# Another order and split of the first blocks, and a later start of GpSimd's gathers, in a kernel of two LoRA layers

## The chip, the cores and the metric

One core of a Trainium2 chip. The metric is the device time of one execution in microseconds (us), the median of the runs of a kernel.

## What is computed

Two dense layers of 1024 x 1024 in float32, each with a residual, a bias and a low-rank term of rank 16 that every one of the 8 batch entries (256 tokens each) chooses from 32 adapters. Cut to what matters:

```python
def layer0(x, ids, W, b, lora_As, lora_Bs):          # lora_As (32, 1024, 16), lora_Bs (32, 16, 1024)
    base = jnp.einsum('bti,oi->bto', x, W) + b
    h = jnp.einsum('bti,bir->btr', x, lora_As[ids])
    return base + jnp.einsum('btr,bro->bto', h, lora_Bs[ids]) * 2.0
def layer1(x, ids, W, b, A, Bw):                     # A (32, 16, 1024), Bw (32, 1024, 16)
    base = jnp.einsum('bsd,od->bso', x, W) + b
    h = jnp.einsum('bsd,brd->bsr', x, A[ids])
    return base + jnp.einsum('bsr,bor->bso', h, Bw[ids])
x = x + layer0(x, itok_B_0_23, ...)                  # x (8, 256, 1024)
x = x + layer1(x, itok_B_6_15, ...)
```

## The kernel before

With nothing nonlinear between the layers, the kernel multiplies the two weights first: U = W0 transposed plus the identity, V = W1 transposed plus the identity, one product of 1024 x 1024, and then every batch entry is multiplied by that one matrix. Both products are done on quadrants of 512 x 512 with seven products in place of eight (a Strassen-Winograd scheme), so sums and differences of quadrants are made (`us3`, `vt3`, `us4`, ...). A quadrant is held as four row blocks of 128 partitions x 512 columns, side by side in 2048 columns.

Float32 accuracy comes from a split: each operand x is written as a high part (a cast to the matmul's reduced float32, on ScalarE: `high...`) and a low part (x minus the high part, on VectorE: `low...`), and every 128 x 128 x 512 product is three matmuls: `high_pass` (L1065, high by high) and the two `low_passes` (L1069, L1070).

The order within each engine is written out by hand; each engine runs its queue in that order and waits on semaphores.

- **SyncE** (L300 to L309) issues the loads: the four row blocks of `u11` and `v11` in turn, 256 KB each (L302), then the quadrants `u12`, `v21`, `u21`, `v22`, `v12`, `u22`, 1 MB each (L305), then the bias (L309).
- **GpSimd** (L373 to L405) makes the identity (`ident`, L375) and the masks, waits for the adapter numbers, and runs a loop of eight gathers of 64 KB from the table A1T into `a1_raw` (L394, semaphore `lora_landed`; the trace calls that memory g_all), then eight from B0T (L398), then A0 (L405).
- **VectorE** zeroes the warm-up operand (L870), the bias sum (L871) and `t_cols` (L872). For each row block k of u11 and v11 it adds the identity on the diagonal piece in place (`diagonal`, L656) and makes the low parts (`low_first`, L661). Then come the low halves of u12 and v21 (L666), `combine("us3")` of u21 and u11 (L674), the diagonal of v22 (L646), the difference `a_diff` of the two halves of `a1_raw` (L886, waits for all of `lora_landed`), `low_factors(0)` (L679), `combine("vt3")` (L674), the low parts of us3 and vt3 (L671), and so on up to `low("us4")`, `make_e1(0)` (L701) and `low("v22")` (L671).
- **ScalarE** casts the high parts: `high_first` (L431) after the diagonal was added, `high_half` (L435), `high` (L438), and `high_factors(0)` (L443), which also waits for all of `lora_landed`, between `high("us3")` and `high("vt3")`.
- **TensorE** does eight matmuls on zeros (`WARM`, L1105) as soon as VectorE has zeroed their operand, then u11 x v11 row block by row block (L1108 to L1122), u12 x v21 (L1125 to L1139), `gt_passes` with the A1T factors (L1141), us3 x vt3 (L1145 to L1150), four transposes (`turn`, L1091), and us4 x v22 (L1157 to L1161), for which it needs both low parts. Later, for each batch entry, `h_product` (L1258) and seven products (L1227 to L1229).

A name with a slot in `SLOT` shares its place in `ops` with others, and the semaphores `hi` and `lo` of a place count on over all of them; `filled(q, n)` gives the count at which n parts of q are in place, from `PARTS`.

Of the kernel before, what the change touches and what calls it, by code (L numbers as in the profile page):

```python
# [10 lines left out]
P = 128  # L11
HALF = 512
WARM = 8
DMA = 16
# [25 lines left out]
def lora_pair(nc, xT, U11, V11, W0, W1T, A0, B0T, A1T, B1, b0, b1, idx0, idx1, out):  # L40
# [22 lines left out]
    with ExitStack() as ctx:  # L63
# [3 lines left out]
        def sem(name):  # L67
            return ctx.enter_context(nc.semaphore(name))
# [63 lines left out]
        def raw_k(name, k, n=1):  # L132
            return raw(name)[:, k * HALF:(k + n) * HALF]
# [42 lines left out]
        landed = {q: sem(f"landed_{q}") for q in ("u12", "u21", "u22", "v12", "v21", "v22")}  # L176
        first_landed = {q: [sem(f"landed_{q}_{g}") for g in range(KH)] for q in ("u11", "v11")}
        lora_landed = sem("lora_landed")
        b0t_landed = sem("b0t_landed")
# [14 lines left out]
        masks_made = sem("masks_made")  # L194
        bias_zeroed = sem("bias_zeroed")
        diag_added = sem("diag_added")
# [28 lines left out]
        t_summed = sem("t_summed")  # L225
        t_zeroed = sem("t_zeroed")
        t_bounced = sem("t_bounced")
# [41 lines left out]
        def _(sp):  # L269
# [29 lines left out]

            for k in range(KH):  # L300
                for q, src in (("u11", U11), ("v11", V11)):
                    sp.dma_start(raw_k(q, k), src[k, :, :]).then_inc(first_landed[q][k], DMA)  # L302
            for q in ("u12", "v21", "u21", "v22", "v12", "u22"):
# [3 lines left out]
                             ).then_inc(landed[q], DMA)  # L307
            sp.wait_ge(bias_zeroed, 1)
            sp.dma_start(bias_sum[0:1, :], b1).then_inc(bias1_landed, DMA)  # L309
# [3 lines left out]
            sp.dma_start(t_dram, t_sum[:, :]).then_inc(t_bounced, DMA)  # L313
            sp.wait_ge(t_zeroed, 1)
            sp.wait_ge(t_bounced, DMA)
# [56 lines left out]
        def _(pool):  # L372
# [53 lines left out]
        @block.scalar  # L426
        def _(act):
            def high_first(k):
                for n, q in enumerate(("u11", "v11")):
                    act.wait_ge(diag_added, 2 * k + n + 1)  # L430
                    nc.scalar.copy(op_k(q, 0, k), raw_k(q, k)).then_inc(hi[SLOT[q]], 1)  # L431
# [72 lines left out]
            act.dma_start(b0_raw[:, :], b0).then_inc(b0_landed, DMA)  # L504
            for k in range(KH):
                high_first(k)
# [134 lines left out]
        def _(dve):  # L641
# [8 lines left out]
            def diagonal(k):  # L650
                for q in ("u11", "v11"):
                    dve.wait_ge(first_landed[q][k], DMA)
                    if k == 0 and q == "u11":
                        dve.wait_ge(ident_made, 2)
                    block_k = raw_k(q, k)[:, k * P:(k + 1) * P]
                    nc.vector.tensor_tensor(block_k, block_k, ident[:, :], ALU.add).then_inc(diag_added, 1)  # L656

            def low_first(k):
                for q in ("u11", "v11"):
                    dve.wait_ge(hi[SLOT[q]], filled(q, k + 1))  # L660
                    nc.vector.tensor_tensor(op_k(q, 1, k), raw_k(q, k), op_k(q, 0, k), ALU.subtract  # L661
                                            ).then_inc(lo[SLOT[q]], 1)
# [206 lines left out]

            nc.vector.memset(c_rows[:, 0:HALF].bitcast(F32), 0.0).then_inc(warm_set, 1)  # L870
            nc.vector.memset(bias_sum, 0.0).then_inc(bias_zeroed, 1)  # L871
            nc.vector.memset(t_cols[:, :], 0.0).then_inc(t_zeroed, 1)  # L872
            for k in range(KH):
                diagonal(k)
                low_first(k)
# [3 lines left out]
            dve.wait_ge(landed["u21"], DMA)  # L879
            dve.wait_ge(lo[SLOT["u11"]], filled("u11", KH))  # L880
            combine("us3", "u21", "u11", ALU.subtract)
# [175 lines left out]
        def _(pe):  # L1057
# [50 lines left out]
            for k in range(KH):  # L1108
                pe.wait_ge(hi[SLOT["u11"]], filled("u11", k + 1))
# [4 lines left out]
                pe.wait_ge(lo[SLOT["u11"]], filled("u11", k + 1))  # L1114
                pe.wait_ge(lo[SLOT["v11"]], filled("v11", k + 1))
# [298 lines left out]
```

## Time and profile before

| | us |
|---|---|
| median of 3 runs | 284.11 (284.02 to 284.24) |
| the profiled execution | 284.42 |
| its span, first to last instruction | 282.8 |
| TensorE busy | 278.3 (98%) |
| VectorE busy | 215.2 (76%) |
| ScalarE busy | 102.3 (36%) |
| GpSimd busy | 19.3 (7%) |

The page's name for an engine is PE for TensorE (PEld its weight loads, PEldq the sequencer that feeds it), DVE for VectorE, ACT for ScalarE, POOL for GpSimd, SP for SyncE; a q behind a name is the engine's sequencer. A group with x4 stands for four instructions in a row. A matmul's 0.39 us includes its pipeline; the distance between two starts is what it costs. The page's granted clock reads 9 tenths or more in all slices.

### The profile page before, as it was taken

To read this page: it belongs to the slowest core of one execution; us is meant where nothing else is said; L and a number is where in the kernel's file an instruction comes from. 1 tells how busy PE (TensorE), PEld (TensorE's weight loads), DVE (VectorE), ACT (ScalarE), POOL (GpSimd) and SP (SyncE) were. 2 spreads that over 40 slices of the span, in tenths; PEclk is the share of its full clock that TensorE was granted. 3 is DMA by queue.
4 is the path that set the end of the run, shared out by engine and by line. 5 is a ranking of instruction groups with operands and counts; after the bars stand their busy time and mean duration, and the time that the engine had idled before them with its cause. 6 is when DMAs were issued, how large, how long until landed. Compare 5 with 4: busy or idle time off the path is not lost.

```text
span 282.8 us, 3853 instructions
## 1 busy us (share of the span) xinstructions
PE 278.3 (98%) x1319; PEld 224.5 (79%) x1319; DVE 215.2 (76%) x318; ACT 102.3 (36%) x141; POOL 19.3 (7%) x45
## 2 busy tenths in 40 slices
PE   7999999999999999999999999999999999999995
PEld 5888888888868887877888878888878888878885
DVE  5789999999899899967975873865873875865413
ACT  4565464262965574322331231141221131321100
POOL 3333200400000001000000100000000000000000
PEclk9999999999999999999999999999999999999999
DMA  6997000100365400451622802712701712212002
GB/s 217 391 409 309 31 1 2 57 19 0 129 230 211 139 14 19 158 185 76 206 74 76 261 37 75 236 46 80 249 37 74 239 43 93 75 39 86 25 37 111
DMA packets 13095, 33.92 MB, mean 120 GB/s; under 512 B 2149, under 2 KB 2405, under 8 KB 13078
## 3 DMA queue, kind: packets, MB, share of 16 engines
q1 hardware_dynamic: 11906, 31.60, 31.6%
q0 software_dynamic: 1024, 2.10, 2.3%
q8 instruction: 10, 0.16, 0.2%
q14 instruction: 7, 0.06, 0.1%
q10 hardware_dynamic: 148, 0.00, 0.0%
HBM read 22.09 MB, written 11.60 MB: 119 GB/s over the span
## 4 chain that ended last, share of the span: by engine, by line
PE 98%; DVE 0%; issue 0%
PE bank L1227 18%; PE bank L1228 18%; PE bank L1229 18%; PE bank L1065 9%; PE bank L1069 9%; PE bank L1070 9%; PE bank L1258 3%; PE bank L1234 3%; PE bank L1083 1%; PE bank L1105 1%; PE bank L1097 1%; PE bank L1099 1%; PE bank L1098 1%; PE bank L1085 1%; PE bank L1084 1%; PE bank L1167 1%
## 5 line engine op out<-in xcount | busy, mean ns | idle before, releaser
L1227 PE MATMUL bank<-ops,late 128*128 128x512 f32 x192 | 75.5, 393 | 0.0
L1228 PE MATMUL bank<-ops,late 128*128 128x512 f32 x192 | 74.9, 390 | 0.0
L1229 PE MATMUL bank<-ops,late 128*128 128x512 f32 x192 | 74.8, 389 | 0.0
L1069 PE MATMUL bank<-ops 128*128 128x512 f32 x112 | 43.8, 391 | 0.0
L1070 PE MATMUL bank<-ops 128*128 128x512 f32 x112 | 43.6, 390 | 0.0
L1227 PEld LDWEIGHTS bank<-ops,late 128*128 128x128 f32 x192 | 36.1, 188 | 9.5 <-issue 2.1
L1229 PEld LDWEIGHTS bank<-ops,late 128*128 128x128 f32 x192 | 36.1, 188 | 7.7
L1228 PEld LDWEIGHTS bank<-ops,late 128*128 128x128 f32 x192 | 36.1, 188 | 7.4
L1065 PE MATMUL bank<-ops 128*128 128x512 f32 x112 | 41.1, 401 | 0.0
L484 ACT CAST late<-rows 128x512 fp32r<-128x512 f32 x24 | 14.7, 622 | 52.3 <-DVE rows L762 26.0
L484 ACT CAST late<-raw_a 128x512 fp32r<-128x512 f32 x24 | 14.8, 624 | 30.6 <-PE bank L1234 21.1
L1065 PEld LDWEIGHTS bank<-ops 128*128 128x128 f32 x112 | 21.4, 192 | 5.1 <-ACT ops L431 0.7
L1070 PEld LDWEIGHTS bank<-ops 128*128 128x128 f32 x112 | 21.2, 189 | 4.5
L1069 PEld LDWEIGHTS bank<-ops 128*128 128x128 f32 x112 | 21.2, 189 | 4.5
L671 DVE TENSOR_TENSOR ops<-raw_a,ops 128x2048 fp32r<-128x2048 f32 x9 | 20.6, 2284 | 0.6 <-ACT ops L438 0.6
L745 DVE TENSOR_TENSOR late<-rows,late 128x512 fp32r<-128x512 f32 x24 | 16.6, 691 | 5.0 <-ACT late L484 4.8
L438 ACT CAST ops<-raw_a 128x2048 fp32r<-128x2048 f32 x9 | 17.2, 1916 | 6.7 <-DVE raw_a L674 3.6
L745 DVE TENSOR_TENSOR late<-raw_a,late 128x512 fp32r<-128x512 f32 x24 | 16.3, 687 | 3.8 <-ACT late L484 3.7
L849 DVE TENSOR_TENSOR raw_a<-bank,raw_a 128x512 f32<-128x512 f32 x8 | 5.5, 692 | 17.8 <-PE bank L1234 17.8
L438 ACT CAST ops<-raw_b 128x2048 fp32r<-128x2048 f32 x6 | 11.4, 1916 | 6.8 <-DVE raw_b L674 3.5
L671 DVE TENSOR_TENSOR ops<-raw_b,ops 128x2048 fp32r<-128x2048 f32 x6 | 13.6, 2284 | 0.0
L405 POOL DMA_DIRECT2D a_raw<-A x8 | 4.3, 542 | 130.1 <-DVE aa L790 128.1
(153 smaller groups left out, 379.4 us busy)
## 6 DMA issues: line engine op xcount, KB each, us to landing
raw_a<-xT SPq DMA_DIRECT2D x16, 512.0 KB, 4.8
out<-raw_a SPq DMA_DIRECT2D x27, 256.0 KB, 2.0
a<-rb_rows SPq DMA_DIRECT2D x8, 392.0 KB
raw_a<-W1T SPq DMA_DIRECT2D x2, 1024.0 KB, 12.6
raw_b<-W SPq DMA_DIRECT2D x2, 1024.0 KB, 16.3
rb_rows<-b_hl SPq DMA_DIRECT2D x3, 512.0 KB
rb_rows<-late SPq DMA_DIRECT2D x3, 512.0 KB
raw_a<-U SPq DMA_DIRECT2D x4, 256.0 KB, 4.4
```

The lines of the kernel that those rows point to most:

```text
L438: nc.scalar.copy(op(q, 0), raw(q)).then_inc(hi[SLOT[q]], 1)
L484: nc.scalar.copy(x_op(j, 0), x_raw(j, b)).then_inc(op_hi[j], 1)
L671: nc.vector.tensor_tensor(op(q, 1), raw(q), op(q, 0), ALU.subtract).then_inc(lo[SLOT[q]], 1)
L745: nc.vector.tensor_tensor(x_op(j, 1), x_raw(j, b), x_op(j, 0), ALU.subtract).then_inc(op_lo[j], 1)
L1065: return mm(bank[:, :], left(u, 0, k, m), op_k(v, 0, k), start=(k == 0 and not on_top), stop=False, skip_group_check=on_top)
L1069: mm(bank[:, :], left(u, 0, k, m), op_k(v, 1, k), start=False, stop=False, skip_group_check=on_top)
L1070: return mm(bank[:, :], left(u, 1, k, m), op_k(v, 0, k), start=False, stop=(k == KH - 1), skip_group_check=on_top)
L1227: mm(bank[:, :], hi, t_op(t, 0, k), start=(start and k == 0), stop=False, skip_group_check=not start)
L1228: mm(bank[:, :], hi, t_op(t, 1, k), start=False, stop=False, skip_group_check=not start)
L1229: last = mm(bank[:, :], lo, t_op(t, 0, k), start=False, stop=(k == KH - 1), skip_group_check=not start)
L1234: return mm(bank[:, :], h_stack[b % 2][0:STACK, q * P:(q + 1) * P], rb[b % 2][:, h * HALF:(h + 1) * HALF], start=False, stop=True, skip_gr ...
L1258: last = mm(banks[6 + s][j * CT:(j + 1) * CT, 0:T], aa[:, s, k, :], xr[s][:, 2 * kh:2 * kh + 2, tok], start=(k < TILES), stop=(k >= KT - T ...
```

## The change

The first row block of v11 is issued ahead of that of u11, and u11's is loaded as two halves of 256 columns, with a semaphore for the second (`u11_half_landed`). For block 0, `first_block` on ScalarE casts columns 128 to 511 straight from what landed, u11's in two pieces; `first_block` on VectorE writes the high part of the 128 diagonal columns itself (block plus identity, straight into `op_k`), then adds the identity to the raw block and makes the low parts, u11's in two halves. TensorE's first row block waits for these pieces in turn. As u11 now has five parts, `PARTS`, the counts (`filled("u11", k + 2)`, `first_count`) and the number that `high_first` waits for change with it. The warm-up is four matmuls of 128 columns after a memset of 128 columns, and six of 512 columns after the memset of the rest. Two semaphores of memsets become one. GpSimd waits for row block 1 of u11 and v11 before its loop of gathers from A1T.

```diff
-WARM = 8
+WARM = 6
+WARM_SHORT = 4
-PARTS = {"u11": KH, "v11": KH, "u12": 2, "v21": 2, "d21": KH, "d22": KH}
+PARTS = {"u11": KH + 1, "v11": KH, "u12": 2, "v21": 2, "d21": KH, "d22": KH}
...
-            for k in range(KH):
+            sp.dma_start(raw_k("v11", 0), V11[0, :, :]).then_inc(first_landed["v11"][0], DMA)
+            for n, done in ((0, first_landed["u11"][0]), (1, u11_half_landed)):
+                cols = slice(n * HALF // 2, (n + 1) * HALF // 2)
+                sp.dma_start(raw_k("u11", 0)[:, cols], U11[0, :, cols]).then_inc(done, DMA)
+            for k in range(1, KH):
                 for q, src in (("u11", U11), ("v11", V11)):
                     sp.dma_start(raw_k(q, k), src[k, :, :]).then_inc(first_landed[q][k], DMA)
...
             pool.wait_ge(idx_landed, 2 * DMA)
+            for q in ("u11", "v11"):
+                pool.wait_ge(first_landed[q][1], DMA)
             with pool.Fori(0, B) as b:
...
+            def first_block():                                       # ScalarE
+                act.wait_ge(first_landed["v11"][0], DMA)
+                nc.scalar.copy(op_k("v11", 0, 0)[:, P:HALF], raw_k("v11", 0)[:, P:HALF]).then_inc(hi[SLOT["v11"]], 1)
+                for landed_n, cols in ((first_landed["u11"][0], slice(P, HALF // 2)),
+                                       (u11_half_landed, slice(HALF // 2, HALF))):
+                    act.wait_ge(landed_n, DMA)
+                    nc.scalar.copy(op_k("u11", 0, 0)[:, cols], raw_k("u11", 0)[:, cols]).then_inc(hi[SLOT["u11"]], 1)
...
+            def first_block():                                       # VectorE
+                dve.wait_ge(ident_made, 2)
+                for q in ("v11", "u11"):
+                    dve.wait_ge(first_landed[q][0], DMA)
+                    nc.vector.tensor_tensor(op_k(q, 0, 0)[:, 0:P], raw_k(q, 0)[:, 0:P], ident[:, :], ALU.add
+                                            ).then_inc(diag_added, 1)
+                for n, (q, cols) in enumerate((("v11", slice(0, HALF)), ("u11", slice(0, HALF // 2)))):
+                    block = raw_k(q, 0)[:, 0:P]
+                    nc.vector.tensor_tensor(block, block, ident[:, :], ALU.add).then_inc(diag_added, 1)
+                    dve.wait_ge(diag_added, n + 3)
+                    dve.wait_ge(hi[SLOT[q]], 1)
+                    nc.vector.tensor_tensor(op_k(q, 1, 0)[:, cols], raw_k(q, 0)[:, cols], op_k(q, 0, 0)[:, cols],
+                                            ALU.subtract).then_inc(lo[SLOT[q]], 1)
+                cols = slice(HALF // 2, HALF)
+                dve.wait_ge(hi[SLOT["u11"]], 2)
+                nc.vector.tensor_tensor(op_k("u11", 1, 0)[:, cols], raw_k("u11", 0)[:, cols], op_k("u11", 0, 0)[:, cols],
+                                        ALU.subtract).then_inc(lo[SLOT["u11"]], 1)
...
-            nc.vector.memset(c_rows[:, 0:HALF].bitcast(F32), 0.0).then_inc(warm_set, 1)
+            for cols in (slice(0, P), slice(P, HALF)):
+                nc.vector.memset(c_rows[:, cols].bitcast(F32), 0.0).then_inc(warm_set, 1)
...
             pe.wait_ge(warm_set, 1)
+            for _ in range(WARM_SHORT):
+                mm(banks[7][:, 0:P], c_rows[:, 0:P], c_rows[:, 0:P], start=True, stop=True)
+            pe.wait_ge(warm_set, 2)
             for _ in range(WARM):
                 mm(banks[7][:, :], c_rows[:, 0:P], c_rows[:, 0:HALF], start=True, stop=True)
...
+            pe.wait_ge(diag_added, 2)
+            pe.wait_ge(hi[SLOT["v11"]], 1)
+            for m in range(KH):
+                if m % 2 == 0:
+                    pe.wait_ge(hi[SLOT["u11"]], m // 2 + 1)
+                high_pass("u11", "v11", a_banks[m], m, 0)
+            pe.wait_ge(lo[SLOT["v11"]], 1)
+            for m in range(KH):
+                if m % 2 == 0:
+                    pe.wait_ge(lo[SLOT["u11"]], m // 2 + 1)
+                low_passes("u11", "v11", a_banks[m], m, 0)
```

## Rows read from the trace of the kernel before

**Rows 1.** The page: busy times, and the shares of the chain that ended last.

```profile
PE 278.3 (98%) x1319; PEld 224.5 (79%) x1319; DVE 215.2 (76%) x318; ACT 102.3 (36%) x141; POOL 19.3 (7%) x45
...
PE 98%; DVE 0%; issue 0%
```

**Rows 2.** Timeline, 0 to 10 us: start, length, engine, line, operation.

```profile
1.16 0.48 DVE L870 MEMSET c_rows<- 128x512 f32 x1 [1.16 <-PEq L1404]
1.70 3.78 PE L1105 MATMUL bank<-c_rows 128*128 128x512 f32 x8 [1.70 <-DVE c_rows L870]
3.81 0.29 DVE L656 TENSOR_TENSOR raw_a<-raw_a,ident 128x128 f32<-128x128 f32 x1 [1.08 <-DMA raw_a<-U]
4.13 0.62 ACT L431 CAST ops<-raw_a 128x512 fp32r<-128x512 f32 x1 [0.64 <-DVE raw_a L656]
4.42 0.29 DVE L656 TENSOR_TENSOR raw_b<-raw_b,ident 128x128 f32<-128x128 f32 x1 [0.32 <-DMA raw_b<-V]
5.50 2.05 PE L1065 MATMUL bank<-ops 128*128 128x512 f32 x4
6.73 0.29 DVE L656 TENSOR_TENSOR raw_b<-raw_b,ident 128x128 f32<-128x128 f32 x1 [0.34 <-DMA raw_b<-V]
9.41 1.08 PE L1065 MATMUL bank<-ops 128*128 128x512 f32 x4
```

**Rows 3.** GpSimd: entry of the loop, gathers, landing times (all of L394; the one of 19.28; all of L398).

```profile
L392 POOLq MOVE  x1: 29/29/29, 3.7 to 3.7; - x1
5.45 0.68 POOL L394 DMA_DIRECT2D g_all<-A1T  x1 [2.64 <-issue]
16.23 0.53 POOL L394 DMA_DIRECT2D g_all<-A1T  x1 [0.99 <-issue]
DMA to landing us min/median/max: 5.0/5.1/6.1
19.28 0.53 POOL L398 DMA_DIRECT2D rows<-B0T  x1 [1.00 <-issue]
DMA to landing us min/median/max: 5.1/5.1/5.1
DMA to landing us min/median/max: 2.0/4.0/5.1
```

**Rows 4.** Timeline around the factors, and SyncE's load of u21 with its landing.

```profile
5.95 0.52 SPq L305 DMA_DIRECT2D raw_b<-W  x1
DMA to landing us min/median/max: 12.6/12.6/12.6
18.58 2.29 DVE L674 TENSOR_TENSOR raw_a<-raw_b,raw_a 128x2048 f32<-128x2048 f32 x1
22.72 1.04 ACT L443 CAST a<-g_all 128x1024 fp32r<-128x1024 f32 x1
23.80 1.23 DVE L679 TENSOR_TENSOR a<-g_all,a 128x1024 fp32r<-128x1024 f32 x1 [0.26 <-ACT a L443]
24.94 2.28 DVE L674 TENSOR_TENSOR raw_b<-raw_b,raw_a 128x2048 f32<-128x2048 f32 x1
```

**Rows 5.** VectorE's busy time by window, and the entry of us4 x v22.

```profile
20.00:60.00 40.00, 39.54 (x44) 1.00 0.24 86
42.52 2.28 DVE L671 TENSOR_TENSOR ops<-raw_a,ops 128x2048 fp32r<-128x2048 f32 x1
L1160 PEldq EVENT_SEMAPHORE  x1: 2202/2202/2202, 42.6 to 42.6; - x1
45.19 0.48 PE L1065 MATMUL bank<-ops 128*128 128x512 f32 x1
```

**Rows 6.** Timeline at the first h_product.

```profile
109.88 0.22 DVE L790 COPY aa<-g_all 128x128 f32<-128x128 f32 x1
110.55 0.59 PEld L1258 LDWEIGHTS bank<-raw_a,aa 128*32 128x32 f32 x16 [0.35 <-issue]
```

More of the change, by code:

```diff
@@ L177, in lora_pair @@
         first_landed = {q: [sem(f"landed_{q}_{g}") for g in range(KH)] for q in ("u11", "v11")}
+        u11_half_landed = sem("u11_half_landed")
         lora_landed = sem("lora_landed")
@@ L194, in lora_pair @@
         masks_made = sem("masks_made")
-        bias_zeroed = sem("bias_zeroed")
+        zeroed = sem("zeroed")
         diag_added = sem("diag_added")
@@ L225, in lora_pair @@
         t_summed = sem("t_summed")
-        t_zeroed = sem("t_zeroed")
         t_bounced = sem("t_bounced")
@@ L307, in _ @@
                              ).then_inc(landed[q], DMA)
-            sp.wait_ge(bias_zeroed, 1)
+            sp.wait_ge(zeroed, 1)
             sp.dma_start(bias_sum[0:1, :], b1).then_inc(bias1_landed, DMA)
@@ L313, in _ @@
             sp.dma_start(t_dram, t_sum[:, :]).then_inc(t_bounced, DMA)
-            sp.wait_ge(t_zeroed, 1)
+            sp.wait_ge(zeroed, 2)
             sp.wait_ge(t_bounced, DMA)
@@ L504, in _ @@
             act.dma_start(b0_raw[:, :], b0).then_inc(b0_landed, DMA)
-            for k in range(KH):
+            first_block()
+            for k in range(1, KH):
                 high_first(k)
@@ L652, in diagonal, with first_count @@
                     dve.wait_ge(first_landed[q][k], DMA)
-                    if k == 0 and q == "u11":
-                        dve.wait_ge(ident_made, 2)
                     block_k = raw_k(q, k)[:, k * P:(k + 1) * P]
                     nc.vector.tensor_tensor(block_k, block_k, ident[:, :], ALU.add).then_inc(diag_added, 1)
+            def first_block():
[15 more added lines that the diff above has]
+                                        ALU.subtract).then_inc(lo[SLOT["u11"]], 1)
+            def first_count(q, k):
+                return filled(q, k + PARTS[q] - KH + 1)
             def low_first(k):
                 for q in ("u11", "v11"):
-                    dve.wait_ge(hi[SLOT[q]], filled(q, k + 1))
+                    dve.wait_ge(hi[SLOT[q]], first_count(q, k))
                     nc.vector.tensor_tensor(op_k(q, 1, k), raw_k(q, k), op_k(q, 0, k), ALU.subtract
@@ L868, in put_c12 @@
                 nc.vector.tensor_tensor(c12[b % 2], W[:, :], u4[b % 2], ALU.add).then_inc(made["c12"], 1)
-            nc.vector.memset(c_rows[:, 0:HALF].bitcast(F32), 0.0).then_inc(warm_set, 1)
-            nc.vector.memset(bias_sum, 0.0).then_inc(bias_zeroed, 1)
-            nc.vector.memset(t_cols[:, :], 0.0).then_inc(t_zeroed, 1)
-            for k in range(KH):
+            for cols in (slice(0, P), slice(P, HALF)):
+                nc.vector.memset(c_rows[:, cols].bitcast(F32), 0.0).then_inc(warm_set, 1)
+            nc.vector.memset(bias_sum, 0.0).then_inc(zeroed, 1)
+            nc.vector.memset(t_cols[:, :], 0.0).then_inc(zeroed, 1)
+            first_block()
+            for k in range(1, KH):
                 diagonal(k)
@@ L879, in _ @@
             dve.wait_ge(landed["u21"], DMA)
-            dve.wait_ge(lo[SLOT["u11"]], filled("u11", KH))
+            dve.wait_ge(lo[SLOT["u11"]], first_count("u11", KH - 1))
             combine("us3", "u21", "u11", ALU.subtract)
@@ L1103, in _ @@
             pe.wait_ge(warm_set, 1)
+            for _ in range(WARM_SHORT):
+                mm(banks[7][:, 0:P], c_rows[:, 0:P], c_rows[:, 0:P], start=True, stop=True)
+            pe.wait_ge(warm_set, 2)
             for _ in range(WARM):
                 mm(banks[7][:, :], c_rows[:, 0:P], c_rows[:, 0:HALF], start=True, stop=True)
-            for k in range(KH):
-                pe.wait_ge(hi[SLOT["u11"]], filled("u11", k + 1))
+            pe.wait_ge(diag_added, 2)
[9 more added lines that the diff above has]
+                low_passes("u11", "v11", a_banks[m], m, 0)
+            for k in range(1, KH):
+                pe.wait_ge(hi[SLOT["u11"]], filled("u11", k + 2))
                 pe.wait_ge(hi[SLOT["v11"]], filled("v11", k + 1))
@@ L1113, in _ @@
                         high_pass("u11", "v11", a_banks[m], m, k)
-                pe.wait_ge(lo[SLOT["u11"]], filled("u11", k + 1))
+                pe.wait_ge(lo[SLOT["u11"]], filled("u11", k + 2))
                 pe.wait_ge(lo[SLOT["v11"]], filled("v11", k + 1))
```

2 lines of the change are left out of this document (1 added, 1 removed).

## The prediction

> **What bounds the kernel now.** I read the page's busy times and chain first. TensorE is busy 278.3 of 282.8 us and holds 98% of the chain that ended last, so in a first reading the time is the number of matmuls times their spacing, plus whatever delays TensorE [rows 1]. Two questions follow: what keeps TensorE from starting, and which wait along the way has little room, because a shift of any feeder by more than that room reaches the end.
>
> The start is in the timeline of the first 10 us [rows 2]. A VectorE memset of 512 columns (0.48 us) releases eight warm-up matmuls at 1.70; the first block of u11 has landed at 3.81, where VectorE adds its diagonal, ScalarE casts it, and the same for v11; the first real matmul runs at 5.50. Four matmuls from there take 2.05 us (0.43 apart, the lower of the two clock levels, 1.2 GHz), four at 9.41 take 1.08 us (0.23 apart after the 0.39 of the last: the upper level, 2.4 GHz). In between, no gap is left: TensorE has work from 5.50 on.
>
> The second question needs three more views. VectorE is busy 39.54 us of the 40 between 20 and 60 us [rows 5]: it has no room there, so a late start of it at 20 arrives whole at 60. The row of the matmul sequencer at L1160 shows a wait of 2.20 us from 42.6: TensorE's instruction stream stood at the operand `v22` until 44.85, that is until VectorE's `low("v22")` ended (42.52 + 2.28 = 44.80), while matmuls queued ahead of it kept the array busy; the array took the next row block at 45.19 [rows 5]. The room is 45.19 - 44.85 = 0.34 us, less about 0.05 for the way from a release to a matmul. I take 0.3 us. A second narrow place is the first `h_product`: VectorE writes its operand until 109.88 + 0.22 = 110.10, the array wants it at 110.55 [rows 6].
>
> **The change part by part.**
>
> Warm-up. The memset is split; 128 columns are done first. 512 columns cost 0.48 us [rows 2]; 128 cost 0.12 by columns alone and no more than 0.48. I take 0.16, near the columns, so TensorE begins at about 1.38 instead of 1.70 (1.34 to 1.70). Four short matmuls and six of 512 columns follow. The six take 6 x 0.43 = 2.6 us. The short ones have no row at the lower level: between nothing and 0.43 each; their share of columns (a quarter) says 0.11, and 0.4 for four. The warm-up ends near 4.4, at most 5.7 (then it covers the gain of the next step, and TensorE starts no earlier).
>
> First blocks. v11 is issued first and lands where the first DMA landed, 3.81; u11 follows in two halves of 128 KB, of which the first is there before the time at which the second DMA was used, 4.4. ScalarE no longer waits for the diagonal: it casts 384 columns of v11, then 128 of u11. A cast of 512 columns is 0.62 us [rows 2]; by columns alone the two are 0.47 + 0.16, with a full instruction's time each 1.24. First real matmul between 4.5 and 5.1; I take 4.75, the nearer to the columns, as casts grow with them. VectorE's two diagonal pieces (0.29 each) lie beside this; its two further adds and the split low parts end by about 6.5, and TensorE asks for them after four high passes, 4.75 + 1.7 = 6.45. That is covered.
>
> What it is worth: TensorE is 0.75 us early at the lower level, 0.75 / 0.43 = 1.7 matmuls, which later cost 0.23 each: a lead of 0.4 us (0.2 to 0.5 by the ends above; 0.75 if the upper level came earlier by as much, more if it came long before). If the clock came later, the lead would turn into a delay; from 1.38 to the upper level TensorE is no less busy than before, so I put little on that.
>
> SyncE issues nine instead of eight first DMAs, 0.47 us more before each later one. Those are queued behind transfers in any case (u21, issued at 5.95, lands 12.6 us later, 18.55) [rows 4], so I cost it at nothing; without that cover it is 0.47 us.
>
> The GpSimd hold. This is the part that decides. Before, GpSimd's loop over the eight A1T gathers is entered at 3.7 and issues its first at 5.45, 1.75 later, the last at 16.23: 10.78 for seven periods, a pace that is register code and DMA issue and not transfers [rows 3]. Now it waits for u11 and v11 block 1. VectorE waited for v11's block 1 and started on it at 6.73 [rows 2], so the release comes at 6.7 (6.1 to 7.2: the new order can move it by about one block). The first gather goes out at 6.7 + 1.75 = 8.5, the last at 8.5 + 10.8 = 19.3, 3.0 us later than now. How long does it take to land? The eight A1T gathers took 5.0 to 6.1 us (the last, issued at 16.23, 5.0), and the B0T gather issued at 19.28, the very time of interest, took 5.1 [rows 3]. So the last lands at 24.3. Everything queued behind it on GpSimd (B0T, A0) shifts by 3 us too. 19.28 is the second gather of B0T; the last comes six periods of 1.53 later, at 28.5, with the hold at 31.5, and lands by 36.6. Its reader on VectorE stands behind `low("v22")`, which starts at 42.52 [rows 5]: hidden.
>
> Who waits for A1T: VectorE at `a_diff` (between 20.9 and 23.8) and ScalarE at `high_factors(0)` (22.72), whose output VectorE's `low_factors(0)` needs at 23.80 and behind which `vt3` (24.94) and all the rest of its queue stands [rows 4]. A landing at 21.2 left 1.5 us of room; at 24.3 ScalarE starts at 24.35 instead of 22.72, VectorE's row at 23.80 moves to 25.4: VectorE is 1.6 us late. With the bounds of the release (6.1 to 7.2) and of the loop's first pass (its steady 1.53 to 1.75) it is 0.8 to 2.1.
>
> From there no idle time swallows it [rows 5]: `low("v22")` ends at 46.4, the sequencer is released at 46.45, matmuls go on at 46.5 instead of 45.19. The lead of 0.4 is spent waiting. The result does not depend on the lead at all: it is the lateness of VectorE less the room of 0.3, 1.6 - 0.3 = **+1.3 us**. At `h_product` VectorE is 1.6 late and TensorE 1.3, with 0.4 of room: no more is lost. The array idles about 1.7 us near 45 with the upper clock level held; I expect it to stay.
>
> Against the profiled execution (span 282.8, 284.42 with what lies around it): span 284.1, 285.7. That execution is 0.3 above the median of the three, so against 284.11: **285.4**.
>
> **A rule that speaks against this.** The Trainium skill, DMA: Bandwidth & Descriptors, "Anatomy of one DMA — SWDGE (gpsimd) path", gives a fixed 2.0 us plus bytes over 436 GB/s, an estimate of 2.15 us for 64 KB. By it the last gather would land at 21.5, before anyone asks, and the hold would cost nothing. The A1T gathers here took 5.0 to 6.1 us [rows 3], so the trace does not agree at this place; the lowest of B0T, 2.0, does.
>
> **The rivals.**
> 1. *Gathers are quicker than these rows.* If, held back, they landed in 2.0 us, the low of the B0T rows [rows 3], A1T would be there at 21.3 and VectorE would not be late. TensorE's lead of 0.4 then meets the room of 0.3 at L1160: -0.3 us, 283.8. Against it: a gather issued at 19.28, in the same traffic, took 5.1. The rule of the page above would give this case.
> 2. *Faster.* In the same case two gathers fewer (3.0 us at one per 1.53) precede u21, whose landing starts VectorE's chain at 18.58 [rows 4]. 128 KB less over the 256 KB that arrived between the uses of blocks at 3.81 and 4.42 [rows 2] are half of 0.61, 0.3 us, so VectorE has 0.3 + 0.3 of room for TensorE's lead; from a lead above 0.6 on (the clock's upper level sooner) the time is 283.5. It decides only if A1T lands before 22.4, a latency under 3.1 us.
> 3. *A short hold.* Block 1 lands by 6.1 and the loop's first pass takes the steady 1.53 instead of 1.75: VectorE 0.8 late, +0.5, 284.6.
> 4. *More than forecast.* Block 1 lands late, or the DMAs over DRAM that VectorE sets off later land later than in proportion and `h_product` waits too: +2.0, 286.1.
>
> **How the numbers follow.** A tell-apart bound of this kernel is 0.2%, 0.57 us. Forecast 0.68 (284.8 to 285.9); rival 1 0.07, rival 2 0.06, rival 3 and all between it and the forecast 0.11, rival 4 0.08. Faster: rival 2, 0.06. Within 0.2%: rivals 1 and 3, 0.18. Slower: 0.68 + 0.08 = 0.76. The range leaves out rivals 1 and 2 and half of 4: 284.2 to 286.0.
>
> **What would show it.** Right: first gather issued near 8.5, last A1T near 19.3, landing 5 us later; VectorE idle about 1.5 us before `a_diff` (released by a DMA into g_all); `low("v22")` ending near 46.4; TensorE idle over 1 us just before L1065 at 46.5, and no other idle. First real matmul near 4.75. Wrong: VectorE not idle at 22 to 24 us, or gaps elsewhere on VectorE between 25 and 45 that take the delay up, or TensorE continuous through 45.

## The result

The changed kernel took 286.54 us (median of 6 runs, 286.07 to 287.59); the kernel before took 284.25 (6 runs, 284.02 to 285.07) beside it. The ratio is 1.0080, with a 95% interval of 1.0063 to 1.0097: slower by 0.8%. The forecast was 285.4 with a range of 284.2 to 286.0. Sign and mechanism came as written; the size lies outside the range. The profiled execution took 286.61 us with a span of 285.0, 2.2 us above the span of before, where +1.3 had been forecast.

### The profile page after: what moved, and what is told of

It reads as the page before. It is cut to its first block, busy times and chain, and to the rows that moved or that the text cites. A ratio compares the mean times of both kernels' runs of the same rounds, so it can differ in the third digit from the quotient of the medians.

```text
span 285.0 us, 3866 instructions
## 1 busy us (share of the span) xinstructions
PE 278.2 (98%) x1321; PEld 224.2 (79%) x1321; DVE 215.8 (76%) x322; ACT 102.0 (36%) x142; POOL 19.2 (7%) x45
## 2 busy tenths in 40 slices
DMA packets 13241, 33.95 MB, mean 119 GB/s; under 512 B 2165, under 2 KB 2677, under 8 KB 13222
## 4 chain that ended last, share of the span: by engine, by line
PE 59%; DVE 2%; issue 0%
PE bank L1283 18%; PE bank L1284 18%; PE bank L1285 18%; PE bank L1314 3%; PE bank L1290 3%; DVE ops L711 1%; PE bank L1346 0%; PE bank L1347 0%; PE bank L1345 0%; DVE ops L778 0%; DVE raw_a L780 0%; DVE g_all L735 0%; DVE raw_a L902 0%; PE bank L1348 0%; DVE aa L830 0%; DVE aa L828 0%
## 5 line engine op out<-in xcount | busy, mean ns | idle before, releaser
L711 DVE TENSOR_TENSOR ops<-raw_a,ops 128x2048 fp32r<-128x2048 f32 x9 | 20.6, 2285 | 0.1
L711 DVE TENSOR_TENSOR ops<-raw_b,ops 128x2048 fp32r<-128x2048 f32 x6 | 13.6, 2284 | 0.0
```

The costliest lines, as they stand in the source:

```text
L711: nc.vector.tensor_tensor(op(q, 1), raw(q), op(q, 0), ALU.subtract).then_inc(lo[SLOT[q]], 1)
```

## The profile after, and how it reads

First the page of the changed kernel: busy times, and the first line of the chain that ended last.

```profile
PE 278.2 (98%) x1321; PEld 224.2 (79%) x1321; DVE 215.8 (76%) x322; ACT 102.0 (36%) x142; POOL 19.2 (7%) x45
...
PE 59%; DVE 2%; issue 0%
```

TensorE's busy time is what it was (278.3) [rows 1]; 2.2 us of idle time came in. Its share of the chain fell from 98% to 59%: the chain does not follow TensorE back to the start any more, it leaves it for VectorE, at the first `h_product` (112.79 us). So TensorE now waits somewhere for VectorE, and the question is where and why; the chain alone does not say how much was lost there and how much before it.

The timeline of the first 8 us, changed kernel (start, length, engine, line, operation, and in brackets the idle time before it with what ended it):

```profile
1.08 0.57 DVE L911 MEMSET c_rows<- 128x128 f32 x2 [1.08 <-PEq L1460]
1.30 1.12 PE L1147 MATMUL bank<-c_rows 128*128 128x128 f32 x4 [1.30 <-DVE c_rows L911]
2.22 2.87 PE L1150 MATMUL bank<-c_rows 128*128 128x512 f32 x6
...
3.65 0.51 ACT L441 CAST ops<-raw_b 128x384 fp32r<-128x384 f32 x1
4.06 0.29 ACT L445 CAST ops<-raw_a 128x128 fp32r<-128x128 f32 x1
4.89 1.60 PE L1107 MATMUL bank<-ops 128*128 128x512 f32 x4
5.24 0.41 ACT L445 CAST ops<-raw_a 128x256 fp32r<-128x256 f32 x1 [0.88 <-DMA raw_a<-U]
...
7.40 0.29 DVE L674 TENSOR_TENSOR raw_b<-raw_b,ident 128x128 f32<-128x128 f32 x1 [0.33 <-DMA raw_b<-V]
```

The start does what the change says. The warm-up begins at 1.30 instead of 1.70, the first real matmul at 4.89 instead of 5.50 [rows 2]. It is the warm-up that it waits for, not its operands: the last cast that it needs ended at 4.06 + 0.29 = 4.35, and the last warm-up matmul started at 4.46, one spacing of 0.43 before 4.89. The block of v11 that GpSimd's wait names is there by 7.40, not by 6.7. Then GpSimd's gathers from A1T, changed kernel: entry of the loop (sequencer), first and last gather, and time to land of the eight.

```profile
L401 POOLq EVENT_SEMAPHORE  x1: 43/43/43, 7.4 to 7.4; - x1
L402 POOLq MOVE  x1: 29/29/29, 7.5 to 7.5; - x1
9.26 0.67 POOL L404 DMA_DIRECT2D g_all<-A1T  x1 [6.44 <-issue]
20.03 0.53 POOL L404 DMA_DIRECT2D g_all<-A1T  x1 [1.00 <-issue]
DMA to landing us min/median/max: 4.9/5.1/5.5
```

The semaphore was passed at 7.4 (7.38 in the record), as VectorE started on the same block. The first gather went out at 9.26, 1.88 after the release, the last at 20.03, and that one landed 5.05 later, at 25.08. Who was waiting for it stands in the waits view (engine, tile and line, what it waited for: us in total, times, longest) and in VectorE's timeline:

```profile
DVE factor_sums L928 <- DMA g_all<-A1T: 2.9, 1, 2.9
ACT a L462 <- DMA g_all<-A1T: 2.8, 1, 2.8
```

```profile
18.04 2.29 DVE L714 TENSOR_TENSOR raw_a<-raw_b,raw_a 128x2048 f32<-128x2048 f32 x1 [0.35 <-DMA raw_b<-W]
...
25.17 0.69 DVE L928 TENSOR_TENSOR factor_sums<-g_all 128x512 f32<-128x512 f32 x1 [2.89 <-DMA g_all<-A1T]
26.19 1.23 DVE L719 TENSOR_TENSOR a<-g_all,a 128x1024 fp32r<-128x1024 f32 x1 [0.32 <-ACT a L462]
27.33 2.29 DVE L714 TENSOR_TENSOR raw_b<-raw_b,raw_a 128x2048 f32<-128x2048 f32 x1
```

VectorE had begun `us3` 0.54 us earlier than before (18.04, before 18.58), then stood 2.89 us for A1T, and comes out late: L719 at 26.19 answers to 23.80, `vt3` at 27.33 to 24.94 [rows 4], 2.39 late both. Follow that number down the queue, on VectorE and then on TensorE, changed kernel:

```profile
32.88 0.39 PE L1127 MATMUL bank<-ops,a 128*128 128x512 f32 x1
34.16 0.47 PE L1107 MATMUL bank<-ops 128*128 128x512 f32 x1 [0.89 <-DVE ops L711]
...
45.17 0.60 PE L1133 MATMUL bank<-ident,g_all 128*128 128x128 f32 x4
47.31 0.47 PE L1107 MATMUL bank<-ops 128*128 128x512 f32 x1 [1.54 <-issue]
```

```profile
44.92 2.28 DVE L711 TENSOR_TENSOR ops<-raw_a,ops 128x2048 fp32r<-128x2048 f32 x1
...
L1216 PEldq EVENT_SEMAPHORE  x1: 2205/2205/2205, 45.0 to 45.0; - x1
...
112.79 0.59 PEld L1314 LDWEIGHTS bank<-raw_a,aa 128*32 128x32 f32 x16 [0.48 <-DVE aa L830]
```

`low("v22")` starts at 44.92 instead of 42.52 [rows 5]: 2.40 late, so the 2.39 of L719 has gone through 18 us of VectorE's queue without losing anything. It ends at 47.20, the sequencer is let go at 45.0 + 2.205 = 47.25, and the array goes on at 47.31, which answers to 45.19: 2.12 late. The room of 0.3 is all that was taken off: 2.40 - 0.3 = 2.1. At `h_product` the array starts at 112.79 instead of 110.55 [rows 6], 2.24 late, and the span is 2.2 longer. So `h_product` took another 0.1: its operand was 2.63 late, and its own room of 0.4 [rows 6] did not cover that any more. Of the 0.23 by which VectorE fell further behind between the two places, a wait that the kernel before does not have may be the cause, VectorE of the changed kernel:

```profile
87.16 2.29 DVE L714 TENSOR_TENSOR raw_a<-raw_b,raw_a 128x2048 f32<-128x2048 f32 x1 [0.42 <-DMA rb_rows<-b_hl]
```

TensorE's own early start ends in the first of the two rows that show idle time. The matmul before 34.16 started at 32.88 and the next was due 0.23 later, at 33.11; before, the same one ran at 33.95. TensorE was 0.84 us ahead there and waited all of it away, for the low part of `vt3` (L711, 31.73 to 34.02).

## What the runs were to tell apart

The theory: GpSimd's hold moves the landing of A1T, that makes VectorE late, and VectorE's lateness less a room of 0.3 us is the loss; the rest of the change is worth nothing in either direction. The rivals: that the new first blocks cost something themselves (a ninth DMA, other landings); that the hold hurts in another way than through A1T (the gathers from B0T and A0 behind it, `h_product`); that the hold brings the big loads in earlier, so that a kernel which uses its time well comes out ahead of before.

### The two halves of the change: no_hold and hold_only

no_hold is the changed kernel without GpSimd's two waits; hold_only is the kernel before with them.

```diff
             pool.wait_ge(idx_landed, 2 * DMA)
-            for q in ("u11", "v11"):                  # no_hold: away; hold_only: added to the kernel before
-                pool.wait_ge(first_landed[q][1], DMA)
             with pool.Fori(0, B) as b:
```

> The changed kernel without GpSimd's two waits; all else of the change stays. Theory T (the hold makes A1T late, ScalarE's factor cast and VectorE's queue behind it start 2.4 us late, TensorE stands at us3 x vt3 and us4 x v22): the first gather is issued near 5.5, A1T has landed by 21.5, no VectorE wait before the difference of the factors, and the time is that of the kernel before less TensorE's lead as far as its room of 0.3 us lets it through: 283.7 to 284.2. Rival R (the split first blocks and the new load order cost the time: block 1 lands at 7.4 instead of 6.7, and more small steps on VectorE): at least half of the loss stays, 285.3 or more.

> The kernel before with nothing but GpSimd's wait for row block 1 of u11 and v11. T: these land at 6.7 in the old load order, the first gather goes out near 8.6 (1.9 after the release, as measured in the changed kernel), the last near 19.4, landed by 24.4; ScalarE's factor cast starts at 24.4 instead of 22.7, VectorE is 1.7 late, less the room of 0.3: +1.4, 285.6. R: 284.5 or less, as the hold is harmless.

no_hold took 284.81 us (12 runs), before 284.42: ratio 1.0021 (1.0010 to 1.0033), span 282.8. hold_only took 286.30 (6 runs): 1.0079 (1.0055 to 1.0103), span 283.9. So the hold alone makes the loss of the whole change (1.0080), within intervals that leave room for half a microsecond, and all the rest makes 0.2% by itself. Both came out above what had been expected: no_hold 0.6 us above the upper end of 283.7 to 284.2, so the new start costs something where it was to gain a little, and hold_only 0.7 above 285.6. The rival's bounds (285.3 or more without the hold, 284.5 or less with it alone) were both missed. VectorE, in order no_hold and hold_only, at `a_diff` and `low_factors(0)`:

```profile
23.11 0.69 DVE L925 TENSOR_TENSOR factor_sums<-g_all 128x512 f32<-128x512 f32 x1
24.06 1.23 DVE L716 TENSOR_TENSOR a<-g_all,a 128x1024 fp32r<-128x1024 f32 x1 [0.26 <-ACT a L459]
```

```profile
24.13 0.69 DVE L888 TENSOR_TENSOR factor_sums<-g_all 128x512 f32<-128x512 f32 x1 [1.88 <-DMA g_all<-A1T]
25.14 1.23 DVE L681 TENSOR_TENSOR a<-g_all,a 128x1024 fp32r<-128x1024 f32 x1 [0.32 <-ACT a L445]
```

Without the hold `a_diff` waits for nothing; with it, in the old order of loads, VectorE stood 1.88 us. In hold_only the first gather went out at 8.23 and A1T landed at 24.04: 1.0 us sooner than in the changed kernel, because its block 1 was there sooner. That is nearly the case the prediction worked out (first gather 8.5, landing 24.3), and its span is +1.04 where +1.3 was forecast.

In no_hold TensorE's early start is lost already at 17.3 us, where it waits for v21 (L1104, timeline of no_hold):

```profile
17.32 1.43 PE L1104 MATMUL bank<-ops 128*128 128x512 f32 x5 [0.94 <-issue]
```

### The dose: hold_block0 and hold_block2

The changed kernel with the hold on row block 0, and on row block 2, in place of 1.

```diff
-                pool.wait_ge(first_landed[q][1], DMA)
+                pool.wait_ge(first_landed[q][0], DMA)     # hold_block0; hold_block2: [q][2]
```

> The changed kernel with the hold on row block 0 in place of 1. Block 0 of u11's first half landed at 3.9, the adapter numbers are there at 3.7: the gathers start within 0.4 us of where they do without a hold, and A1T lands more than 1 us before it is wanted. T: the time of the kernel without a hold, within 0.2 us. A theory by which any wait on GpSimd costs a fixed amount: 1 us or more above it.

> The changed kernel with the hold on row block 2, which landed at 8.7 where block 1 landed at 7.4: 1.34 us later. T: past the room, every microsecond of hold is a microsecond of time: A1T lands 1.3 later, near 26.4, VectorE 3.7 late, and the time is 1.3 above the changed kernel: 287.9. If the loss were a fixed price of the hold, or bounded by another wait, it stays at 286.5.

hold_block0: 284.94 us (10 runs), ratio 1.0018 (0.9998 to 1.0038), span 283.2. hold_block2: 288.92 (4 runs), 1.0155 (1.0124 to 1.0187), span 287.2. The first is 0.13 us from no_hold, as expected; the second is 1.0 above the 287.9 expected. VectorE of hold_block2:

```profile
27.50 0.69 DVE L928 TENSOR_TENSOR factor_sums<-g_all 128x512 f32<-128x512 f32 x1 [5.41 <-DMA g_all<-A1T]
28.51 1.23 DVE L719 TENSOR_TENSOR a<-g_all,a 128x1024 fp32r<-128x1024 f32 x1 [0.32 <-ACT a L462]
```

A1T landed at 27.41 there, 2.33 us after its landing in the changed kernel, and the span is 2.18 longer. Only 1.10 of the 2.33 is the hold (last gather issued at 21.13 instead of 20.03); the other 1.23 is that this last gather took 6.28 us to land instead of 5.05. From hold_only to the changed kernel it is 1.04 and 1.15. Once VectorE waits for A1T at all, each microsecond that A1T is later is a microsecond of the kernel.

### Giving VectorE other work in the wait: hold_factors_later, hold_refill, before_refill

In hold_factors_later VectorE makes `vt3` and the low part of `us3` first and takes `a_diff` after `low("vt3")`. In hold_refill it goes further: `low("us3")`, `vt3`, `low_factors(0)`, `a_diff`, `low("vt3")`. before_refill is the same order without a hold and without the rest of the change.

```diff
+            low("us3")
+            dve.wait_ge(landed["v12"], DMA)
+            combine("vt3", "v12", "v22", ALU.subtract)
+            low_factors(0)
             dve.wait_ge(lora_landed, B * DMA)
...
-            low_factors(0)
-            dve.wait_ge(landed["v12"], DMA)
-            combine("vt3", "v12", "v22", ALU.subtract)
-            low("us3")
             low("vt3")
```

> The changed kernel, hold and all, but VectorE takes the A1T work behind other work: vt3, low factors, low us3, low vt3, and the difference of the factors last. A1T still lands near 25.1. Theory T (all of the loss is VectorE's lateness, and it stands in front of A1T with work behind it that doesn't need A1T): vt3 starts when v12 has landed, 23.9, in place of 27.3; low v22 ends about 0.8 later than in the kernel before in place of 2.4; time +0.5 in place of +2.2: 284.9. Rival S (the late gathers cost because ScalarE or TensorE itself needs the factors then): TensorE's wait moves to the factor passes and the time stays above 286.

> The changed kernel with VectorE's idle stretch before A1T filled: low us3, vt3, low factors, difference, low vt3. By T VectorE starts low us3 at 22.3 when its high part is there, vt3 at 24.5, the factors at 26.7 (ScalarE's cast ends at 26.2), low vt3 at 28.7: it ends 0.7 earlier than in the kernel before, because the hold brought u21 in 0.5 earlier (18.0 for 18.55) and now nothing waits for A1T. TensorE waits a little at the factor passes (27.9) and keeps 0.5 to 0.7 of its lead: 283.6 to 283.9, 0.15 to 0.25% faster than before. If TensorE needs the factors earlier than I think, or the hold has another cost, 284.5 or more.

> The same new VectorE order in the kernel before, with neither hold nor new first blocks: control for the order alone. There VectorE has no idle stretch to fill (A1T lands at 21.2, wanted at 22.7), so T says no gain: the low factors come at 28.5, just when TensorE wants them, and the time is 284.2 to 284.8. A gain of 0.5 us or more would say that the order, not the hold, is what helps in the run above.

hold_factors_later: 285.46 us (10 runs), 1.0043 (1.0026 to 1.0060), span 283.5. hold_refill: 284.80 (12 runs), 1.0022 (1.0007 to 1.0038), span 283.4. before_refill: 284.51 (12 runs), 1.0007 (0.9989 to 1.0025), span 283.1. The kernel before took 284.30 in these. A1T landed at 24.97 in hold_refill, as late as in the changed kernel (25.08), and the loss fell from 0.8% to 0.2%, which is what no_hold loses too (1.0021). VectorE and the factor passes on TensorE in hold_refill:

```profile
23.25 2.29 DVE L711 TENSOR_TENSOR ops<-raw_a,ops 128x2048 fp32r<-128x2048 f32 x1
...
27.66 1.22 DVE L719 TENSOR_TENSOR a<-g_all,a 128x1024 fp32r<-128x1024 f32 x1
28.93 0.50 PE L1125 MATMUL bank<-ops,a 128*128 128x512 f32 x1 [0.50 <-DVE a L719]
```

VectorE does not wait for A1T any more, its `low("v22")` is 0.39 us late instead of 2.40. TensorE waits 0.50 for the late factors, out of its lead. So the hold hurts through A1T at VectorE's queue and nearly by that alone. hold_factors_later gets only half of the loss back, 0.6 us above its expectation: VectorE's `low("v22")` is 1.02 us late there, as it stood 1.20 us for v12 before `vt3` (started at 24.21), a stretch that hold_refill fills with `low("us3")`. That hold_refill would come out below the kernel before (283.6 to 283.9 expected) did not happen. That needed u21 to land sooner, and it did not: VectorE started on it at 18.90 in hold_refill, at 18.58 in the kernel before. Over the traces that start is at 17.86, 18.02, 18.04, 18.66, 18.77 and 18.90 with a hold on block 1 or 2, and at 18.52, 18.55, 18.58, 18.75, 18.85, 19.28 and 19.55 with none or a shorter one. The first group is 0.5 us sooner in the mean (18.38 against 18.87), but the two overlap. Part of the overlap is another difference between the kernels, whether u11's block 0 comes in one load or two. With one load it is 18.02 (hold_only) against 18.52 to 18.75 in four traces; with two it is 17.86 to 18.90 with the hold (mean 18.45) against 18.85 to 19.55 without it or with a shorter one (mean 19.23). That the hold brings the loads in earlier is therefore likely, from few traces that were not all taken side by side, and it is smaller than what the hold costs.

### A change that was to do nothing: hold_bias_later

The first two bias sums of VectorE, which stand ahead of `low("us4")`, moved behind `low("v22")`, in the changed kernel. They are 2.73 us of VectorE (four instructions from 39.47 on, L749), and without them `low("v22")` might come sooner.

```diff
             dve.wait_ge(summed["vt3"], 1)
-            bias_first(0)
-            bias_first(1)
             dve.wait_ge(m1_kept, KH)
             low("us4")
...
+            bias_first(0)
+            bias_first(1)
             bias_first(2)
```

> The changed kernel with four VectorE steps that nobody waits for soon (the first four bias sums, 2.7 us) moved from ahead of low us4 and low v22 to behind them. The wait at us4 x v22 then has 2.7 us more room and disappears. If that wait alone were the bound, the time falls by its 1.6 us, to 285.0. T in its full form says VectorE's queue is one chain from the A1T landing to the first h_product at 112 us, with the same work in it: the stall comes back there, about 1.5 us before L1314, and the time stays at 286.3 to 286.7.

It took 289.03 us (4 runs), ratio 1.0173 (1.0143 to 1.0203), span 286.0, where 286.3 to 286.7 had been expected: a plain miss. Timeline of hold_bias_later, VectorE and TensorE:

```profile
41.09 2.29 DVE L711 TENSOR_TENSOR ops<-raw_a,ops 128x2048 fp32r<-128x2048 f32 x1 [2.00 <-ACT ops L457]
...
43.90 2.28 DVE L711 TENSOR_TENSOR ops<-raw_a,ops 128x2048 fp32r<-128x2048 f32 x1
...
113.76 0.42 PE L1314 MATMUL bank<-raw_a,aa 128*32 128x256 f32 x4 [1.70 <-DVE aa L830]
```

The bias sums had filled the 2.0 us in which VectorE waits for ScalarE's cast of `us4`. Taken from there, they leave an idle stretch behind, so that 2.73 us moved away bring `low("v22")` in by 1.0 only (half of which is A1T, landed 0.47 sooner here), and most of them comes back as work further down: VectorE is 1.38 late at `low("v22")` and 3.60 late at the first `h_product`, 2.22 more, where the changed kernel had 0.23 more. So the second narrow place [rows 6] decides and the span is 3.1 longer. Work that stands in a wait is free there; moved to where the queue is full, 2.0 of its 2.7 us were paid.

### The gathers behind A1T: hold_b0t_only

no_hold, with the gathers from B0T alone held until v22 has landed. The first B0T gather goes out at 23.62; in the kernel before it went out at 17.75 (the 19.28 of [rows 3] is the second). GpSimd, kernel before and hold_b0t_only:

```profile
17.75 0.53 POOL L398 DMA_DIRECT2D rows<-B0T  x1 [0.98 <-issue]
```

```profile
23.62 0.54 POOL L406 DMA_DIRECT2D rows<-B0T  x1 [6.81 <-issue]
```

```diff
+            pool.wait_ge(landed["v22"], DMA)               # ahead of the loop over B0T, in no_hold
```

> The changed kernel with its hold taken from the A1T loop and a longer one put before the next loop, B0T: GpSimd waits there until v22 has landed (near 21.5), so B0T goes out some 5 us later than without any hold, while A1T goes out at once. T (it is the lateness of A1T's readers that costs): B0T is read after 40 us, lands by 37, and the time is that of the kernel without a hold, 284.6 to 285.0. If holding GpSimd costs by itself, 286 or more.

285.21 us (10 runs), before 284.62: ratio 1.0015 (0.9996 to 1.0033), span 283.5. That is 0.2 us above the range expected and no more above the kernel before than no_hold is. A1T was on time there (21.51). The gathers from B0T can go out 5.9 us late at next to no cost (in the changed kernel they are 3.8 late, at 21.55), so the loss of the hold is not theirs.

### The new start by itself: no_hold_one_load and warm_up_alone

no_hold_one_load is no_hold with block 0 of u11 loaded by one DMA of 256 KB, for which both of ScalarE's casts of u11 wait. warm_up_alone is the kernel before with the new warm-up and nothing else.

```diff
-            for n, done in ((0, first_landed["u11"][0]), (1, u11_half_landed)):
-                cols = slice(n * HALF // 2, (n + 1) * HALF // 2)
-                sp.dma_start(raw_k("u11", 0)[:, cols], U11[0, :, cols]).then_inc(done, DMA)
+            sp.dma_start(raw_k("u11", 0), U11[0, :, :]).then_inc(first_landed["u11"][0], DMA)
...
-                                       (u11_half_landed, slice(HALF // 2, HALF))):
+                                       (first_landed["u11"][0], slice(HALF // 2, HALF))):
```

> The changed kernel without the hold, and with u11's first block in one load again (v11 still first, casts and low parts still in pieces). If the ninth load and its 1 KB rows are what made the kernel without the hold 0.2% slower than the one before, this is 284.2 to 284.5; if it is v11 ahead of u11 or the extra VectorE steps, or only that the lead cannot be used, it stays at 284.7 to 284.9.

> The kernel before with the new warm-up alone (128 columns zeroed first, four short matmuls, six long). The first warm-up matmul comes at 1.3 in place of 1.7, the first real one stays at 5.5. No stage behind it is bound by TensorE's start: 284.1 to 284.6, the time of the kernel before.

no_hold_one_load: 284.44 us (12 runs), 0.9988 (0.9973 to 1.0003), span 282.7. warm_up_alone: 284.81 (12 runs), 1.0015 (0.9995 to 1.0034), span 282.5. Before: 284.62. The first is as expected, warm_up_alone 0.2 us above its range. The intervals of no_hold (1.0010 to 1.0033) and of no_hold_one_load do not overlap: the second load of u11's block costs about 0.3%, and is what made no_hold slower. (The two were not run side by side; each is measured against its own runs of the kernel before.) The traces show a way: VectorE started on u21 at 18.52 to 18.75 in the four traces with one load and no hold on block 1 or 2, and at 18.85, 19.28 and 19.55 in the three with the split load, and all that stands behind u21 in its queue is later with it. No kernel here is clearly below the one before; the nearest is no_hold_one_load, whose interval includes 1.

### The thirteen traces side by side

From the profiled execution of each kernel, in us. "VectorE late" is the start of `low("v22")` less 42.52, and the start of the first of the two copies that make the first `h_product`'s operand less 109.74, its start in the kernel before; "TensorE late" is less 110.55.

| kernel | first A1T gather | A1T landed | VectorE late at v22 | VectorE late at h_product | TensorE late at h_product | span less that of before |
|---|---|---|---|---|---|---|
| before | 5.45 | 21.21 | 0 | 0 | 0 | 0 |
| warm_up_alone | 5.26 | 21.17 | -0.05 | -0.63 | -0.35 | -0.35 |
| before_refill | 5.22 | 21.02 | 0.05 | 0.05 | 0.21 | 0.21 |
| no_hold | 5.38 | 21.15 | 0.28 | 0.40 | 0.00 | -0.03 |
| no_hold_one_load | 5.37 | 21.75 | 0.19 | -0.12 | -0.12 | -0.14 |
| hold_b0t_only | 5.50 | 21.51 | 0.98 | 0.71 | 0.68 | 0.68 |
| hold_block0 | 5.98 | 22.29 | 0.72 | 0.27 | 0.41 | 0.39 |
| hold_only | 8.23 | 24.04 | 1.36 | 1.22 | 1.04 | 1.04 |
| hold_bias_later | 8.92 | 24.61 | 1.38 | 3.60 | 3.21 | 3.14 |
| hold_factors_later | 9.19 | 25.03 | 1.02 | 0.91 | 0.70 | 0.69 |
| hold_refill | 9.23 | 24.97 | 0.39 | 0.62 | 0.56 | 0.54 |
| after | 9.26 | 25.08 | 2.40 | 2.63 | 2.24 | 2.19 |
| hold_block2 | 10.35 | 27.41 | 4.72 | 4.65 | 4.39 | 4.37 |

In each row whose span is over half a microsecond longer, the span grows by the larger of the two VectorE columns less 0.3 to 0.46 us (0.08 in hold_refill). Below that the rows scatter by as much as they say. Where VectorE did not wait for A1T, what it is late by (0.98 in hold_b0t_only, 0.72 in hold_block0) comes with u21, on which it started at 19.55 and 19.28 instead of 18.58.

The timed runs agree on the order, but not always on the size: hold_only lost 1.9 us in the median against 1.04 in its trace (its six spans go from 283.9, the profiled one, to 285.7), hold_block2 4.5 against 4.37. The release moves from run to run, as the next section shows, and one trace is one draw of it.

## Why the prediction was right, and where its size failed

**The bound and the two narrow places: right.** VectorE carried its lateness whole from 26 to 45 us (2.39 and 2.40), L1216 was where the array lost it, with 2.2 us of sequencer wait in both kernels, and the room of 0.3 held. `h_product` as the second narrow place showed itself in hold_bias_later.

**The sign, and the hold as the part that decides: right.** hold_only alone gives 1.0079 of 1.0080.

**The term that was mis-sized: VectorE's lateness, 1.6 forecast, 2.40 measured.** Its parts: the release, forecast at 6.7, came at 7.38 (+0.68 us); the first pass of the loop took 1.88 instead of 1.75 (+0.13); the seven periods 10.77 as forecast; the landing 5.05 instead of 5.0 (+0.05). Together 0.86, which covers 2.40 - 1.6 = 0.8 (the forecast had rounded its sums up by 0.05), and makes 2.12 instead of 1.3 at TensorE. The other 0.1 us between the medians (+2.3) is within what one trace says of six runs.

The step that failed is therefore "VectorE waited for v11's block 1 and started on it at 6.73, so the release comes at 6.7 (6.1 to 7.2)", and with it "I cost it at nothing" for SyncE's ninth DMA. The load of that block, SyncE's rows in the kernel before and in the changed kernel, each with its landing:

```profile
2.37 0.43 SPq L302 DMA_DIRECT2D raw_b<-V  x1
DMA to landing us min/median/max: 4.3/4.3/4.3
```

```profile
2.84 0.43 SPq L309 DMA_DIRECT2D raw_b<-V  x1
DMA to landing us min/median/max: 4.5/4.5/4.5
```

u11's block 0 takes two DMAs now, so v11's block 1 is the fifth instead of the fourth and is issued 0.47 us later. That is the 0.47 of the prediction, which counted on the transfers queued ahead to cover it; nothing covered it. The other 0.2 is that this load took 4.54 us from issue to landing instead of 4.34.

The rest of the traces agree. Block 1 of v11 was there at 6.71, 6.35, 7.22, 7.27 and 6.87 with u11's block 0 in one load (the last with v11 issued first), and at 7.38, 6.85, 7.34, 7.17, 7.32, 7.03, 7.36 and 7.46 with the split. From issue to landing it took 4.0 to 4.9 us in the first group (mean 4.5) and 4.0 to 4.6 in the second (mean 4.4), so the later issue makes the whole of the shift between the means, 6.9 to 7.2. The scatter of about 0.9 us between executions with the same loads stays open; against it one row was too little, and the bound of 7.2 was drawn too near: seven of the thirteen traces lie above it.

The split shows in the rate of the loads too. The windows view of 4 to 5 us (time, busy time of each engine, granted clock, DMA share, GB/s by the packets that began in it), kernel before and changed kernel:

```profile
4.00:5.00 1.00, 1.00 (x4) 0.66 (x2) 0.60 (x3) 0.87 (x2) 0.00 (x0) 1.00 1.04 266
```

```profile
4.00:5.00 1.00, 1.00 (x4) 0.76 (x3) 0.96 (x4) 0.36 (x2) 0.00 (x0) 1.00 1.13 81
```

Over the traces it is 218 to 375 GB/s in the five with one load and 81 to 185 in the eight with the split: the groups do not meet. Why the rate drops so far is not shown.

**The landing of a gather under load: right, and it carried the argument.** The rule of the Trainium skill, DMA: Bandwidth & Descriptors, "Anatomy of one DMA — SWDGE (gpsimd) path", gave rival 1 an estimate of 2.15 us for 64 KB; the eight held gathers took 4.9 to 5.5 us. They were issued while 1 MB loads were under way, and the kernel's own rows gave the figure to take. By the rule A1T would have landed at 20.03 + 2.15 = 22.2; it landed at 25.08.

**The gain of the start: right that it is worth nothing, wrong in where it goes.** The first matmul came at 4.89 (forecast 4.75, bounds 4.5 to 5.1), and that this is near has luck in it. The forecast had the warm-up over by 4.4 and the casts as the bound; the casts were done by 4.35, and the warm-up kept TensorE until 4.89, in the main because its four short matmuls cost 0.22 to 0.27 us each instead of 0.11. The lead was 0.84 us by the end of the factor passes, not 0.4, since the upper clock level (2.4 GHz, 0.23 us between matmuls instead of 0.43) came sooner: at 7.78 in the trace of before, where TensorE had worked since 1.70, and at about 5.8 in that of the changed kernel, where it had worked since 1.30. Two matmuls of the changed kernel at the upper level:

```profile
6.32 0.39 PE L1111 MATMUL bank<-ops 128*128 128x512 f32 x1
6.55 0.39 PE L1112 MATMUL bank<-ops 128*128 128x512 f32 x1
```

It came between 5.4 and 7.9 over the traces. The lead was then waited away whole at 34.16, where the forecast had no idle time; the sum was not touched, since it had been built on VectorE's lateness alone.

**"No other idle", and nothing more lost at `h_product`: wrong.** Besides the stretch ahead of 47.31, TensorE idled 0.89 us ahead of 34.16 for the low part of `vt3`. Its room can be read off before: that low part was ready 2.39 earlier, at 31.63, and asked for at 33.95. A lateness of 2.40 just exceeds 2.3 and a lead of 0.84 comes on top. What has room for a lateness of 1.6 has none for 2.4, and the same holds at `h_product`, which took 0.1 more.

**The rivals.** Rival 1 (quick gathers) and rival 2 (faster) fell with the landing of 5.05 us; rival 2's other half, that fewer gathers bring u21 in sooner, held in this trace (18.04 instead of 18.58) and is likely over all. Rival 3 (a short hold) needed a block 1 there by 6.1, which no trace has; the nearest is hold_only's, 6.35 and +1.04. Rival 4 (more, +2.0) is nearest to what happened: through its first half, a late block 1, and in a small part through its second, the wait at 87.16 and the 0.1 at `h_product`. It had been given 0.08, and the range left out half of it.

**The ninth DMA of SyncE, costed at nothing:** besides the 0.47 us at the release, no_hold against no_hold_one_load says 0.3%, 0.9 us; the cover of queued transfers did not hide a further DMA among the first. In the changed kernel no such cost shows on top of the hold's loss: hold_only without it measures the same (1.0079 against 1.0080), within intervals of about 0.2% either way.

## What to carry to other kernels

A wait that is put ahead of a loop of gathers moves the last gather's landing by the same amount; find who reads that landing and how much room that reader's queue has before the bounding engine asks for its result. The loss is that lateness less the narrowest room behind it, and a head start of the bounding engine gives none of it back. When the release of such a wait is a DMA's landing in the crowded first microseconds, take its spread over several traces, not the one row at hand, and add what each DMA issued ahead of it costs (0.47 us here); and when a queue is full, look for the work beside each of its waits before moving a piece out, for that piece may be standing in a wait.

## What was not expected of the hardware

- With u11's first block in two loads of 128 KB instead of one of 256 KB, the loads moved 81 to 185 GB/s between 4 and 5 us (eight traces) instead of 218 to 375 (five traces), and v11's block 1, issued 0.47 us later, landed 0.4 us later in the mean.
- One and the same load, the 256 KB of v11's block 1, took 4.0 to 4.9 us from issue to landing over the thirteen traces.
- One more DMA among the first (two of 128 KB in place of one of 256 KB) cost about 0.3% of the kernel (1.0021 against 0.9988, in two series).
- TensorE's upper clock level came between 5.4 and 7.9 us in executions whose warm-up had begun at 1.3 to 1.7.
